# Queries, two mixtures and attention: from four phases to one program in steps

## What is computed

```
x = x + ttt(layernorm(x))        # gradient and Newton-Schulz steps, then the queries
x = x + mixture(layernorm(x))
x = x + attention(layernorm(x))  # 16 heads of 64, mask by frames of 32 tokens
x = x + mixture(layernorm(x))    # the same weights once more

# end of ttt
h_q = swish(q @ gate) * (q @ val)          # 128 -> 512
o   = h_q @ proj @ proj_w + proj_b

# mixture: 8 experts, the best 2 of each token
gates = softmax(x @ Wg + bg); top2, their gates divided by their sum
out   = sum over the two of gate * (x @ We[e] + be[e])
```

## Time and profile before

| what | value |
|---|---|
| median of 3 runs | 866.03 us (865.5 to 868.25) |
| the profiled execution | 866.14 us |
| its span, first to last instruction | 863.7 us |
| mean granted PE clock | 0.94 of 2.4 GHz |
| PE / DVE / ACT / POOL busy | 90% / 63% / 46% / 31% |
| queries / first mixture (from the trace) | 343 to 393 / 393 to 449 us |
| attention / second mixture | 449 to 806 / 806 to 864 us |

### The profile page before, as it was taken

How to read it: one execution, slowest core, us unless ns; L and a number is a source line. 1 busy time by engine, 2 the same in 40 slices (tenths; PEclk the granted TensorE clock), 3 DMA queues, 4 the chain that set the end, 5 groups by cost and what they waited for, 6 DMA issues and landing times. The chain is left out here.

```text
span 863.7 us, 15529 instructions
## 1 busy us (share of the span) xinstructions
PE 774.2 (90%) x5512; PEld 616.6 (71%) x5512; DVE 545.4 (63%) x1649; ACT 394.9 (46%) x1118; POOL 270.7 (31%) x476
## 2 busy tenths in 40 slices
PE   3669999897999988987858999999999999999786
PEld 1239999775999976677645677777777777777765
DVE  3945656444555535664796776776677666665468
ACT  4733333243333234312255766565556555564224
POOL 4830000002445002100372444343334333333027
PEclk9969999997999999895898999999999999999678
DMA  3040000000000000000000000000000000000001
GB/s 104 1 134 1 1 2 1 1 1 1 1 1 2 1 1 1 0 1 1 0 2 0 2 2 2 2 2 1 2 2 1 2 2 2 2 1 2 1 0 50
DMA packets 9466, 7.17 MB, mean 8 GB/s; under 512 B 1584, under 2 KB 9008, under 8 KB 9264
## 3 DMA queue, kind: packets, MB, share of 16 engines
q1 hardware_dynamic: 9392, 6.19, 2.3%
HBM read 5.14 MB, written 1.05 MB: 7 GB/s over the span
## 5 line engine op out<-in xcount | busy, mean ns | idle before, releaser
L1295 POOL TENSOR_SCALAR t_p_<-t_p_,t_rinv_ 128x128 f32<-128x128 f32 (+3 forms) x256 | 132.1, 532 | 202.3 <-DVE t_rinv_ L1491 202.3
L1325 ACT ACTIVATE t_p_<-t_p_,t_nmin_ 128x128 f32<-128x128 f32 (+3 forms) x256 | 140.0, 551 | 9.1 <-DVE t_nmin_ L1484 9.1
L1484 DVE CUSTOM_DVE_ANT_0 t_p_<-t_S_,t_mask_ 128x128 f32<-128x128 f32 (+3 forms) x256 | 112.8, 487 | 21.7 <-PE t_S_ L1382 17.3
L1330 ACT ACTIVATE t_pT_<-t_T_ 128x384 f32<-128x384 f32 (+1 forms) x96 | 50.5, 526 | 118.3 <-PE t_T_ L1394 118.3
L1394 PEld LDWEIGHTS t_T_<-ident,t_p_ 128*128 128x128 f32 x640 | 68.2, 141 | 44.9 <-issue 26.0
L1382 PE MATMUL t_S_<-t_k_,t_q_ 64*128 64x256 f32 (+3 forms) x512 | 95.0, 468 | 0.1
L1394 PE MATMUL t_T_<-ident,t_p_ 128*128 128x128 f32 x640 | 90.8, 281 | 0.3 <-ACT t_pT_ L1330 0.3
L1409 PEld LDWEIGHTS t_O_<-t_pT_,t_v_ 128*64 128x64 f32 x1280 | 69.2, 137 | 11.0 <-ACT t_pT_ L1330 10.5
L1409 PE MATMUL t_O_<-t_pT_,t_v_ 128*64 128x128 f32 x1280 | 76.9, 275 | 0.0
L522 DVE SCALAR_TENSOR_TENSOR g_sw<-g_th,g_G 128x512 f32<-128x512 f32 x32 | 22.0, 688 | 71.3 <-ACT g_slope L436 66.2
L1382 PEld LDWEIGHTS t_S_<-t_k_,t_q_ 64*128 64x128 f32 x512 | 41.5, 185 | 26.9 <-DVE t_nmin_ L1484 12.3
(11 more groups left out here) (259 smaller groups left out, 1794.5 us busy)
## 6 DMA issues: line engine op xcount, KB each, us to landing
wqkv<-in_L_attn_b_w_qkv_dram SPq DMA_DIRECT2D x1, 1536.0 KB
x<-in_L_attn_a_x_dram SPq DMA_DIRECT2D x4, 256.0 KB, 4.2
out_dram<-x SPq DMA_DIRECT2D x4, 256.0 KB, 2.3
we<-in_L_ffn_We_dram SPq DMA_DIRECT2D x1, 512.0 KB
wout<-in_L_attn_b_w_out_dram SPq DMA_DIRECT2D x1, 512.0 KB
proj<-n_L_attn_a_ttt_proj_dram SPq DMA_DIRECT2D x1, 256.0 KB, 5.3
gv<-n_L_attn_a_ttt_gate_dram SPq DMA_DIRECT2D x1, 256.0 KB, 4.9
gv<-in_L_attn_a_ttt_val_dram SPq DMA_DIRECT2D x1, 256.0 KB, 5.4
```

The lines of the kernel that those rows point to most:

```text
L1295: last = pool.tensor_scalar(pr[:, G.par, h, cols], pr[:, G.par, h, cols], rinv[:, G.par, n:n + 1], 1.0, ALU.mult, ALU.mult)
L1325: act.activation(pr[:, G.par, h, cols], pr[:, G.par, h, cols], ACT.Exp, bias=nmin[:, G.par, n:n + 1], scale=-1.0, accum_out=rsum[:, G.par, ...
L1330: act.activation(pT[:, G.par, 0, G.blocks], psT[:, 0, 0:G.width], ACT.Copy).then_inc(t["eA"], 1)
L1484: dve.tensor_tensor_reduce(pr[:, G.par, h, cols], psS[:, (2 * G.n + h) % 3, at_:at_ + keys], mask[:, SEQ - keys:SEQ], 1.0, -NEG, ALU.add, ...
```

## The change

`query_phase`, `moe_phase` and `attention_phase` are replaced by one block, `second_half_phase`. All engines walk over the same numbered steps, -52 to 117, and each kind of work has a table of the steps at which it is due; on every engine the order within a step is fixed. Attention's groups are steps 0 to 95. Queries are chunks at steps -50, -48, ... (gate in one step, val in the next), the answers of a batch in one piece at steps -41, -33, -25, -17. The mixtures are cut into four jobs: first mixture batches 0 and 1 (job 0) and 2 and 3 (job 1), second mixture batches 0 to 2 (job 2) and 3 (job 3). Layer norms go batch by batch, as do transposes, splits and logits; ranking goes by job.

```diff
+    class Job:
+        BATCHES = ((0, 2), (2, 4), (0, 3), (3, 4))
+        TOPS = (-24, -8, 86, 106)
+        FILLS = (tuple(range(-16, -8)), tuple(range(0, 8)),
+                 (96, 97, 98, 99, 99, 101, 102, 102, 103, 105, 105, 106), (108, 108, 108, 111))
+        SUMS = (tuple(range(-16, -8)), tuple(range(0, 8)),
+                (96, 97, 98, 99, 100, 102, 103, 104, 104, 105, 106, 107), (112, 113, 114, 115))
...
+            self.weights = self.top + (5 if j < 2 else 4)
+            self.bias = self.top + (7 if j < 2 else 5)
...
+            QUERY = -50
+            ANSWER = 9
+            Q_STEPS = [-6] + [3 * p for p in range(self.PAIRS - 1)]
+            K_STEPS = [-5] + [3 * p + 1 for p in range(self.PAIRS - 1)]
+            V_STEPS = [-4, -3, -2, -1] + [3 * n + 2 for n in range(2 * BATCH * TPB - TPB)]
+            X_STEPS = [-8] + [IN_BATCH * b + 12 for b in range(BATCH - 1)]
+            OUT_STEPS = [IN_BATCH * b + step for b in range(BATCH)
+                         for step in (17, 18, 19, 20) + ((29, 30, 31, 32) if b < BATCH - 1 else (29, 29, 29, 29))]
+            M_STEPS = [QUERY + 2 * NC * b + 12 for b in range(BATCH)] + [34, 58, 82, 102]
+            N_STEPS = [s + 1 for s in M_STEPS]
+            T_STEPS = [s + (3 if s < 0 else 2) for s in M_STEPS]
+            L_STEPS = [s + (5 if s < 0 else 3) for s in M_STEPS]
+            W_STEPS = [Job(j).weights for j in range(NJ)]
+            B_STEPS = [Job(j).bias + k for j in range(NJ) for k in Job(j).batches]
```

The order within a step, where it matters here:

```diff
 # DVE
+                    if O and O.g == 2: take_o(O.pair)
+                    if G: row_min(G)
+                    if T: take_p(T)
+                    if R: invert(R)
+                    if chunk(s, 1) is not None: hidden(chunk(s, 1))
...
+                    for b in planned(X_STEPS, s + 3): moments(b)
+                    for c in planned(M_STEPS, s): moments(c % BATCH)
+                    for b in planned(X_STEPS, s + 2): norm_x(b)
+                    for c in planned(N_STEPS, s): norm(c)
...
+                    for J in jobs(s, Job.TOPS): shift(J)
+                    for part in range(3):
+                        for J in jobs(s - 1 - part, Job.TOPS): route(J, part)
...
+                    for J, n in tiles(s, Job.summed): accumulate(J, n)

+                def accumulate(J, n):
...
+                    for e in range(4):
+                        acc = (a, b_)[e % 2][:, i % 2, :]
+                        if e == 1:
+                            dve.wait_ge(m["z"], i + 1)
+                        if e > 1:
+                            dve.wait_ge(m["s"], 4 * i + e - 1)
+                        so_far = (x[:, J.row(n), :], z[:, i % 2, :])[e] if e < 2 else acc
+                        dve.scalar_tensor_tensor(acc, bank("el", i)[:, tile_of(e)], weight(e), so_far,
+                                                 ALU.mult, ALU.add).then_inc(m["s"], 1)
 # POOL
+                    if R: normalize(R)
+                    for b in planned(X_STEPS, s + 3): power("a", b, b)
+                    for c in planned(M_STEPS, s): power("m", c, c % BATCH)
...
+                    for J, n in tiles(s - 1, Job.summed): close(J, n)
+                    for J, n in tiles(s, Job.weighed): add_experts(J, n)

+                def add_experts(J, n):
+                    i = J.index(n)
+                    pool.wait_ge(m["y"], i + 1)
...
+                    pool.tensor_tensor(half[:, :, :], y[:, i % 2, 0:2, :], y[:, i % 2, 2:4, :], ALU.add).then_inc(m["z0"], 1)
+                    pool.wait_ge(m["z0"], i + 1)
...
+                    pool.tensor_tensor(z[:, i % 2, :], half[:, 0, :], half[:, 1, :], ALU.add).then_inc(m["z"], 1)
 # ACT
+                    take_p(T), exps(G), high_q, swish, take_q, take_x, high, gates, high_weights
+                    for J, n in tiles(s, Job.weighed): weigh(J, n)
 # PE
+                    scores(G), turn(T), widen (gate, val), project q, k, v, output, turn_x,
+                    turn_tokens, logits, turn_weights, biases, experts upper, experts lower,
+                    answer, weigh(O.pair)
```

More of the change, by code:

```diff
@@ new lines, in chunk, with jobs, tiles @@
+            def chunk(s, lag=0):
+                n, odd = divmod(s - QUERY - lag, 2)
+                return n if not odd and 0 <= n < BATCH * NC else None
+            def jobs(s, steps):
+                return [Job(j) for j in planned(steps, s)]
+            def tiles(s, when):
+                return [(Job(j), n) for j in range(NJ) for n in range(Job(j).nt) if when(Job(j), n) == s]
+            spare, last_use = {}, {}
+            free = [psS[:, 0, :], psS[:, 1, :], psS[:, 2, :], psT[:, 0, :], psT[:, 1, :]]
@@ L1429, in _ @@
+                for s in STEPS:
                     G, T, O = at(s, 0), at(s, LT), at(s, LV)
+                    if s == QUERY - 1:
+                        fold()
                     if G:
@@ L1446, in _ @@
+                    for J, n in tiles(s, Job.lower):
+                        experts(J, n, "el", 0, m["E"])
+                    if query(s, ANSWER) is not None:
+                        answer(query(s, ANSWER))
                     if O and O.g == 2:
-                        for g in range(self.NG):
-                            weigh(Group(O.n - 2 + g))
-                for m in range(TPB):
-                    output(BATCH - 1, m)
+                        weigh(O.pair)
             @block.vector
@@ L1552, in hybrid_block_kernel @@
+                    for J, n in tiles(s, Job.summed):
+                        accumulate(J, n)
 def hybrid_block_kernel(nc, *tensors):
```

974 lines of the change are left out of this document (519 added, 455 removed).

## The result

The changed kernel takes **890.28 us** (median of 4 runs, 888.88 to 893.22) beside 866.69 for the kernel before: ratio 1.0276, 95% interval 1.0244 to 1.0307. It is slower by 2.8%, where 853.3 had been forecast. The profiled execution has a span of 887.1 us, where 863.7 stood before.

The account below looks back on a forecast made before the run. PE taken to bound attention, waits between engines the stretches around it. Early part -0.2, to step 8 -2.9, then PE work +12.8, DVE waits +8, tail -30.4: -12.7 us, 853.3 us; own range 846 to 862, with rivals 836 to 868.

Parts of the forecast that it names:

- (3): Query stage: each next answer is ordered behind the routing of the batch before, 13.2 us apart; answers 1 and 2 by 384.8.
- (5): From the last answer to attention: DVE is full with 31.4 us of work, first row minimum at 435.2.
- The ring: Steps 0 to 7: DVE's sums, POOL's z and normalizing wait on each other in a loop; 46 us for 20.25 before.
- rival A: No ring: ACT and POOL get ahead of the sums, steps 0 to 7 take 31.2 us, total 838.5; chance 0.20.
- The front: All ahead of attention's step 0: first row minimum at 435.2, 28.7 us sooner than before.
- Rival B: PE's work between 394 and 435 runs at half clock, adding 12.4 us, total 865.7; sign: clock under 0.8; chance 0.14.
- Steps 8 to 94: Rest of attention, PE bound: 12.8 us more PE work and 8 us of waits for DVE.
- rival C: DVE's queue stops PE in attention, all 28 us paid instead of 8, total 873.3; chance 0.16.
- The tail: Behind attention, from the last group's row minimum to the end: 46.8 us instead of 77.2, 30.4 us sooner.

Follow-up runs that it names:

- e1: Changed kernel with DVE's sums of the first two jobs' tiles one step after ACT's and POOL's part; 886.2 us, ratio 1.0217.
- e12: Changed kernel with unread matmuls on PE, 14 ahead of each of four query-stage transposes and 4 ahead of two logits; 889.1 us.
- e9: Changed kernel with job 2's sums on DVE one step behind ACT's and POOL's part; 890.4 us, ratio 1.0273.
- e11: Changed kernel with all jobs' sums a step later, job 1 spread over attention, norms in long steps, transposes of batches 0 and 2 later; 857.6 us.
- e14: e11 with POOL's split for batch 3 and its query biases behind the normings, and job 2's ninth tile at step 104 instead of 103; 853.8 us.
- e3: Changed kernel with POOL's power replaced by a multiplication, so the layer norms' scale is not computed; 889.9 us, ratio 1.0265.
- e13: Changed kernel with POOL's query split and bias for batches 2 and 3 waiting for the normings of batches 0 and 1; 890.4 us.
- e15: e14 with 35 unread matmuls in PE's three longest waits of the front; 854.5 us, ratio 0.9863.

## Why the prediction was wrong

**The sign was wrong though the largest term was right.** Two steps failed. The period of an answer in (3) had three terms mis-sized, and in (5) and behind attention DVE's work was added up as if it stood ready, with its waits for POOL's `z` at nothing, where the traces have 8.0 and 12.0 us of them. Point by point:

*The ring, steps 0 to 7.* Forecast 46 us, measured 46.0. Sizes and order were right, and rival A fell. The single steps took 5.1 to 6.8 us, with 5.2 to 6.5 forecast. But the working named one ring, through `z` and the normalizing; e1 showed that with it gone the banks make another of 5.2 us a step, which the prediction did not see. It did no harm to the number, and would have to any advice drawn from it.

*The front, 17.5 us late.* The first answer came 1.4 us sooner than forecast (357.0), so the rest was 18.9 us too slow. What failed first is (3): the period of an answer, 13.2 us, was 16.4 and 16.7. The terms that were mis-sized: power taken 0.3 (with 1.5 as its bound), measured 1.03 (0.7 more); normings taken 1.1, measured 3.05 (1.9 more); matmuls behind the wait at half clock, some 1 us, which the sum had not at all. Together 3.6, for 3.4 missed in each of two periods. The price of a norming beside POOL stood in the prediction's own words, for attention; here it took the 1.11 us of the earlier trace rows, where no operation of POOL is beside. The fourth answer took 20.9 instead of 19, with 5.4 us for its matmuls instead of 3.7. (5), from there to attention 31.4 forecast, 41.6 measured: the sum took DVE as full, and it was busy 28.4 of 42 us. It waited 8.0 us for `z` in this stretch; e1 gave back 5.6 of the 10.2. The prediction had the ring for attention and did not ask for it 30 us earlier, though the order of the engines is the same there. For the other 4.6 us there are normings of 2.0 us beside POOL's adds and the clock (0.50 from 429.4 to 446.5); no run separates them.

*Rival B, the clock.* It was a part and not the whole: 0.81 from 394 to 435, just over the 0.8 that was to be its sign, and 0.50 for another eleven microseconds behind that. B had priced all of 394 to 435 at half clock with 12.4 us. e12 puts the price of the front at 4.2 us, all of it ahead of the fourth answer; behind that answer (411 to 453) no run has taken the clock away.

*Steps 8 to 94, 5.4 us late.* The measured 26.3 us more than before are 11.6 of waits and thus 14.7 of work and clock; the forecast had 8 and 12.8. Of the waits 8.3 us lie where they were expected (steps 35 and 36, 59 and 60, 83 to 90) and 3.1 at steps 8 and 11, where none was; the sum is in the forecast's own range of 3 to 13, and rival C's 28 did not come. For a crowded place 2 us had been taken; the two at steps 35 and 59 cost 2.7 of waiting each, and then a clock of 0.91 over 20 us.

*The tail, 13.0 us late.* The working had three marks, 18.7, 33.6 and 44.1 us behind step 95's row minimum, for PE's last output, the tile behind the first five links of the ranking, and the last closing add. The trace has 21.8, 45.6 and 57.1, so 8.9 of the 13.0 were lost between the first mark and the second. There the working said that the tiles of job 2 fill the waits of the last batch's chain. In the trace they hold it up: their sums stand waiting for `z` (12.0 us in the tail, 5.8 of them there) with the last norm, logits and ranking behind them. Norm and power had the wrong size as in the front (four normings 1.98 us). Some 1.5 us of the forecast's 46.8 stand in no term of its working, so the terms themselves were short by more than 13. e9, e11 and e14 brought 3.6 to 4.9 us; for the 8.1 us that e14 still has over the forecast (54.9 for 46.8) no run shows the cause. Its clock of 0.87 there may be a part.

*The sum.* 851 (the forecast's span) + 17.5 + 5.4 + 13.0 = 887. The bound that the prediction had set itself, 8 us on the way to step 8 and 5 in the tail, was passed in both. e14, with the same work, is 36.5 us faster than the kernel after: front 11 us (106.0 to 94.9), attention 21 (13.2 and 7.7), tail 5. That much was the price of the order of operations and waits, with the clock's changes in it. That its 853.8 us are the 853.3 of the forecast is luck: by the profiled executions e14 is 10.5 us late at step 0 and 8.1 in the tail, and 15.6 us early between, since it has done away with the ring for which the forecast had paid.

## What to carry to other kernels

When phases are laid over each other in one order by steps, price each stretch by the loops and waits that the order makes, not by the work of its fullest engine alone: follow each wait to what stands behind it in the same queue, and look for the next loop (here the PSUM banks) under the first. An operation that takes what two other engines hand on in the same step belongs one step later, behind the operation that the bound engine waits for; light work of a side engine belongs in the long steps. A moved operation must be priced beside its new neighbours: a norming took 0.33 us alone and up to 1.32 beside POOL. And a total that agrees with a forecast says little until its stretches agree.

## What the runs showed of the hardware

- POOL's power of 128x4 elements takes 1.02 us, a multiplication of the same shape 0.20 us (e3).
- Four normings on DVE take 1.11 us alone and 3.05 beside two additions of POOL of 1.30 us each (kernel after, 362.09); the two that meet an addition end with it, the other two take 0.33. With POOL held back the four take 1.11 in the same place (e13).
- Behind the waits of 4.0 to 4.5 us in the front of the kernel after, PE came back at half its clock (1.2 GHz): until 368.0 behind the wait that ends at 365.19, until 409 behind the one that ends at 398.87. From 429.4 to 446.5 the granted clock was 0.50 too, with PE busy for 13.8 of 17.1 us, behind waits of 3.2, 1.5 and 1.3 us. A matmul of 512 columns then takes 0.43 us instead of 0.23. Matmuls that nobody reads kept the clock up (0.94 for 0.89) in e12, and made neither the kernel after (e12) nor e14 (e15) measurably faster.
- The same stretch at half clock cost 1.6 us where it fell on 40 matmuls in a row (e9, 4.03 us for 2.40) and nothing where a wait of PE followed (kernel after).
- Each change of table on ACT (Silu to exponential and back) took 1.3 us: 391.50 to 392.80 and 393.07 to 394.37 in the kernel after, 2.6 together. The Trainium skill ("ScalarE: Activation LUTs", section "What ACT_TABLE_LOAD costs") has 2.66 us for one change, load and drain. The trace shows the load (1.28 us) and no gap before or behind it, so the measured 1.3 us decides here, and the 5 us that the prediction took from the page are twice what was paid.
